# Graph layer and mixture of experts on one core: experts' rows split into 16-bit halves before they are turned

## The reference, cut to what matters

```python
x = x + gnn(layernorm(x), src, dst, edge_weight, ...)     # 3125 nodes x 256, 50000 edges
xt = layernorm(x)
# ffn, 8 experts, D = 256, H = 1024, the best 2 per node
probs = softmax(xt @ Wr + br)
top_p, top_idx = top_k(probs, 2)
weights = top_p / top_p.sum(-1)
xn = (xt - mu) * rsqrt(var + 1e-5)
xe = xn * ln_g[e] + ln_b[e]
h  = gelu(xe @ W1[e] + b1[e])                             # exact gelu
y  = h @ W2[e] + b2[e]
out = x + (weights * y[top_idx]).sum(over the 2)
```

## Time and profile before

| what | value |
|---|---|
| runs | 1226.39, 1227.84, 1229.69 us (median 1227.84) |
| the profiled execution | 1224.0 us |
| its span, first to last instruction | 1222.1 us |
| mean granted TensorE clock over the span | 0.818 |
| busy shares | TensorE 72%, VectorE 62%, GpSimd 54%, ScalarE 43% |

### The profile page before, as it was taken

The page is one execution under the profiler, slowest core; times in us unless marked ns, Lnnn a source line. Parts: engine busy times, 40 slices in busy tenths (PEclk is TensorE's granted clock), DMA queues, the critical chain, the costliest instruction groups (busy, mean ns, idle before and its releaser), DMA issues.

```text
span 1222.1 us, 26281 instructions
## 1 busy us (share of the span) xinstructions
PE 878.2 (72%) x6929; PEld 616.9 (50%) x6930; DVE 760.6 (62%) x1734; ACT 522.3 (43%) x1648; POOL 665.0 (54%) x668
## 2 busy tenths in 40 slices
PE   2284277658676556665579778884399999999994
PEld 1032043335333333333358656774287877877783
DVE  4666079766686556666466774897854555555552
ACT  7983168205463036640011003563055555555552
POOL 3844756564666666766667655351224454454543
PEclk9986589766778578988665769895599999999998
DMA  4114322234232233333444433453112323223231
GB/s 128 65 50 125 103 74 77 81 87 98 84 91 84 83 91 87 91 87 89 124 151 155 122 95 97 148 155 116 34 46 44 51 43 50 45 45 50 43 47 22
DMA packets 59615, 102.51 MB, mean 84 GB/s; under 512 B 10298, under 2 KB 43048, under 8 KB 59400
## 3 DMA queue, kind: packets, MB, share of 16 engines
q0 software_dynamic: 29520, 65.96, 22.4%
q1 hardware_dynamic: 30008, 35.55, 9.3%
HBM read 84.27 MB, written 17.20 MB: 83 GB/s over the span
## 4 chain that ended last, share of the span: by engine, by line
PE 38%; DVE 8%; issue 5%; DMA 1%; another core or an unknown queue 1%; DVEq 1%; ACT 1%; POOL 0%; POOLq 0%; ACTq 0%
PE bank L1061 8%; PE bank L1047 4%; PE bank L1048 4%; PE bank L1049 4%; PE bank L914 4%; PE bank L1063 3%; PE bank L901 2%; PE bank L903 2%; PE bank L902 2%; PE bank L987 1%; PE bank L997 1%; PE bank L1030 1%; DVE RA L1626 1%; DVE small L1694 1%
## 5 line engine op out<-in xcount | busy, mean ns | idle before, releaser
L738 POOL DMA_INDIRECT Wall<-xl_d,gbuf x391 | 396.3, 1013 | 236.3 <-SPq L606 111.4
L1155 ACT ACTIVATE Wall<-Wall 128x128 f32<-128x128 f16 (+1 forms) x782 | 230.3, 385 | 263.0 <-issue 138.2
L901 PE MATMUL bank<-Wall,RB 128*128 x488 | 167.2, 343 | 139.0 <-DVE Wall L1626 95.5
L1626 DVE TENSOR_TENSOR RA<-RA,bank 128x256 f32 x244 | 102.0, 418 | 203.7 <-remote 100.2
L792 POOL DMA_INDIRECT out_dram<-RA,slot_tok x56 | 100.7, 1798 | 163.0 <-ACT RA L1273 144.3
L1267 ACT ACTIVATE RA<-bank,b1T 128x128 f32<-128x128 f32 x448 | 128.1, 369 | 118.8 <-PE bank L1049 118.8
L1047 PE MATMUL bank<-RA,Wall 128*128 128x128 f16 x896 | 174.5, 220 | 0.4 <-issue 0.2
L1048 PE MATMUL bank<-RA,Wall 128*128 128x128 f16 x896 | 174.4, 220 | 0.0
L1049 PE MATMUL bank<-RA,Wall 128*128 128x128 f16 x896 | 174.3, 220 | 0.0
L1061 PE MATMUL bank<-Wall,RA 128*128 x448 | 169.1, 379 | 2.7 <-DVE RA L1905 0.9
L903 PE MATMUL bank<-Wall,RB 128*128 x488 | 167.3, 343 | 4.4 <-issue 4.4
(11 more groups left out here) (337 smaller groups left out, 1523.7 us busy)
## 6 DMA issues: line engine op xcount, KB each, us to landing
stage<-in_L_ffn_W SPq DMA_DIRECT2D x10, 1024.0 KB
Wall<-xl_d,gbuf POOLq DMA_INDIRECT x391
Wall<-in_L_ffn_W SPq DMA_DIRECT2D x6, 1024.0 KB, 6.5
Wall<-in_x SPq DMA_DIRECT2D x4, 640.0 KB, 6.7
xl_d<-Wall SPq DMA_DIRECT2D x4, 640.0 KB
out_dram<-RB SPq DMA_DIRECT2D x4, 640.0 KB
xn_d<-RA SPq DMA_DIRECT2D x4, 640.0 KB
RB<-in_x SPq DMA_DIRECT2D x1, 1792.0 KB
```

The source lines that it names most:

```text
L738: pool.indirect_dma_start(out=ring[:, t % RING * 2 * D:(t % RING + 1) * 2 * D], out_offset=None, in_=xl_d, in_offset=bass.IndirectOffsetOn ...
L901: mm(o, high, ring[:, bass.ds(at, D)], start=True, stop=False)
L1155: last = act.activation(hi_word[:, n % SR, k * S:(k + 1) * S], hi_hot[:, n // HB % 2, n % HB // 2, 0:S, n % 2], ACT.Copy, scale=pay[k][:, ...
L1626: dve.tensor_tensor(a, a, agg_out(n), ALU.add).then_inc(agg_added, 1)
```

## The change

The gathered float32 rows are split before they are turned. `row_highs` on ScalarE copies `xs` to a 16-bit tile; `row_lows` on VectorE subtracts that from `xs` for a second 16-bit tile; `turn` then makes four 16-bit transposes (two blocks of each half) in place of two float32 ones, against a 16-bit identity, into the same PSUM bank seen as 16-bit numbers. `x_high` reads the high halves from PSUM, and `x_low` becomes a plain copy of the low halves. `turn` waits for `row_lows` in place of the gather. The tiles of halves are two deep, in memory that was free. GpSimd makes the 16-bit identity in place of the zeros, once these have been stored.

```diff
+        xh_rows, xl_rows_x = [], []
+        for q in range(2):
+            for lst in (xh_rows, xl_rows_x):
+                lst.append(RA[:, at:at + D // 2].bitcast(F16))
+                at += D // 2
...
+            pool.wait_ge(spare_zeroed, 64)
+            pool.tensor_copy(ident_h, ident[:, :]).then_inc(ident_ready, 1)
             pool.wait_ge(slots_ready, 1)
-            pool.wait_ge(spare_zeroed, 64)
...
-            def turn(t, q, n):
-                pe.wait_ge(xs_in[q], 16 * n)
+            def turn(t, q):
+                pe.wait_ge(rows_lo, t + 1)
                 pe.wait_ge(fx_split, t + 1)
-                for kc in range(KC):
-                    m = nc.tensor.transpose(bank[6 + q % 2][:, kc * P:kc * P + P], xs[q][:, kc * P:kc * P + P], ident[:, :])
+                o = bank[6 + q][:, 0:D].bitcast(F16)
+                for half, rows in enumerate((xh_rows[q], xl_rows_x[q])):
+                    for kc in range(KC):
+                        at = half * D + kc * P
+                        m = nc.tensor.transpose(o[:, at:at + P], rows[:, kc * P:kc * P + P], ident_h)
                 m.then_inc(ft_mm, 1)
...
+            def row_highs(t, q, n):
+                act.wait_ge(xs_in[q], 16 * n)
+                act.wait_ge(ft_mm, t + 1)
+                act.activation(xh_rows[q % 2], xs[q], ACT.Copy).then_inc(rows_hi, 1)
+
             def x_high(t, q):
                 act.wait_ge(ft_mm, 2 + t + 1)
                 act.wait_ge(up_mm, 2 * t + 2)
-                act.activation(xhi[q], bank[6 + q][:, 0:D], ACT.Copy).then_inc(fx_hi, 1)
+                act.activation(xhi[q], bank[6 + q][:, 0:D].bitcast(F16)[:, 0:D], ACT.Copy).then_inc(fx_hi, 1)
...
+            row_highs(0, 0, 1)
+            row_highs(1, 1, 1)
             x_high(0, 0)
             x_high(1, 1)
+            row_highs(2, 2, 1)
             word = expert_word(0)
             gelu(0, 0, word, 0)
+            row_highs(3, 3, 1)
             x_high(2, 0)
             gelu(1, 1, word, 1)
             with act.Fori(0, FT // XR - 1) as i:
...
                     x_high(XR * i + q + 3, (q + 1) % 2)
                     gelu(XR * i + q + 2, q % 2, word, q + 2)
+                    row_highs(XR * i + q + 4, q, i + 2)
                     y_scale(XR * i + q, q % 2)
...
+            def row_lows(t, q):
+                dve.wait_ge(rows_hi, t + 1)
+                dve.tensor_tensor(xl_rows_x[q % 2], xs[q], xh_rows[q % 2], ALU.subtract).then_inc(rows_lo, 1)
+
             def x_low(t, q):
                 dve.wait_ge(fx_hi, t + 1)
-                dve.wait_ge(up_mm, 2 * t + 2)
-                dve.tensor_tensor(xlo[q], bank[6 + q][:, 0:D], xhi[q], ALU.subtract).then_inc(fx_split, 1)
+                dve.tensor_copy(xlo[q], bank[6 + q][:, 0:D].bitcast(F16)[:, D:2 * D]).then_inc(fx_split, 1)
...
             for c in range(2):
                 gate_hots(c)
+            row_lows(0, 0)
+            row_lows(1, 1)
             x_low(0, 0)
             x_low(1, 1)
+            row_lows(2, 2)
...
                     h_parts(XR * i + q + 1, (q + 1) % 2)
                     x_low(XR * i + q + 3, (q + 1) % 2)
+                    row_lows(XR * i + q + 4, q)
                     y_rows(XR * i + q, q % 2, word, q)
```

More of the change, by code:

```diff
@@ L226, in moe_gnn_program @@
             at += D
-        assert at <= NT * D
+        xh_rows, xl_rows_x = [], []
[3 more added lines that the diff above has]
+                at += D // 2
+        assert at <= (NT + 1) * D
         stages = [stage[:, :], f32view(Wall, (NE - 1) * WE // 2, KC * H)]
@@ L249, in moe_gnn_program @@
         zero_h = sb("zero_h", [P, 256], F16)
+        ident_h = zero_h[:, 0:P]
         one_h = sb("one_h", [P, 1], F16)
@@ L427, in moe_gnn_program @@
         ft_mm = sem("ft_mm")
+        ident_ready = sem("ident_ready")
+        rows_hi = sem("rows_hi")
+        rows_lo = sem("rows_lo")
         fx_hi = sem("fx_hi")
@@ L1085, in _ @@
             assert HC == 8
-            turn(0, 0, 1)
-            turn(1, 1, 1)
+            pe.wait_ge(ident_ready, 1)
+            turn(0, 0)
+            turn(1, 1)
             ex = experts(0)
@@ L1096, in _ @@
             m.then_inc(gates_mm, 1)
-            turn(2, 2, 1)
+            turn(2, 0)
             up(1, 1, ex[1])
@@ L1103, in _ @@
                 for q in range(XR):
-                    turn(XR * i + q + 3, (q + 3) % XR, i + 1 + (q + 3) // XR)
+                    turn(XR * i + q + 3, (q + 3) % 2)
                     up_and_down(XR * i + q + 2, q % 2, ex[q + 2], XR * i + q, q % 2, ex[q])
@@ L1109, in _ @@
                 if t + 3 < FT:
-                    turn(t + 3, (t + 3) % XR, (t + 3) // XR + 1)
+                    turn(t + 3, (t + 3) % 2)
                 if t + 2 < FT:
@@ L1927, in _ @@
             h_parts(0, 0)
+            row_lows(3, 3)
             x_low(2, 0)
```

## The result

The changed kernel took **1396.66 us** in the median of 4 runs (1395.71 to 1398.82), against 1228.76 us (1226.39 to 1229.84) for the kernel before: a ratio of 1.137, with a 95% interval from 1.135 to 1.140. It is slower, as forecast, but by 168 us where 113 were forecast, and it lies above the range of 1310 to 1390 us. The profiled executions are one each: 1395.71 us of the changed kernel, near its median, and 1224.0 us of the one before, 4.8 us under its median.

A forecast was written before the change was run, and what follows sets the result against it. TensorE was taken to bound the expert stage. 2.16 us a tile by 52 is 112.3, plus 1.2 for the stage's start: 113.5 us on 1224.0 gives 1337.5, and 3.8 to the median gives 1341 us; range 1310 to 1390.

The forecast's parts named there:

- What bounds the kernel: Expert stage: TensorE, busy 49.7 of 50 us at clock 1.00, is the bound; a tile takes 5.65 us.
- the new wait: Each of the loop's 52 turns waits for row_lows, behind row_highs, behind the last GELU half: +112.3 us.
- The ring's length: Expert loop, one turn to the next through TensorE, ScalarE and VectorE: 7.81 us a tile against 5.65; bounds 7.21 and 8.36.
- the term for TensorE's sequencer: After each turn in the loop, TensorE's register work and waits, hidden before, add 0.35 of a possible 0.63 us.
- the sum: Whole kernel: 112.3 us in the loop and 1.2 us before it make 113.5 us more.
- The turn itself: TensorE's transposes in each tile: four 16-bit ones take 0.22 us, two float32 ones 0.21; nothing gained.
- The third rival: Each transpose has a fixed price: four end 0.55 us later per tile, 29 us in all, 1370 us; chance 0.05.
- The fourth rival: Expert loop: halves ready a tile ahead, turns wait for nothing, 5.65 us a tile or 0.1 less; 1224 us, chance 0.04.
- x_high, x_low, gather, GpSimd: Expert stage: x_high and x_low gain or cost nothing, the earlier gather costs nothing, GpSimd's identity falls in its wait.
- The opening: Start of the expert stage: up(0) starts about 1.2 us later; nothing else is lengthened up to the loop.
- the second rival: TensorE's clock falls in the expert stage, 1.3 us a tile: half the tiles 34 us, 1375 us; all 1409; chance 0.28.
- the sum's bounds: Whole kernel: loop bounds of +81 and +141 us give 1310 to 1370 us.

The follow-up runs named there:

- The first experiment: The changed kernel with row_highs of tile T+4 moved ahead of the GELU of tile T+2, likewise for tile 3 before the loop: 1230.06 us.
- the last one: The kernel before with one wait added: in the loop, turn(T+3) waits for both GELU halves of tile T+1; 1315.50 us.
- the second experiment: The changed kernel with 12 extra matmuls of 256 columns, read by nobody, ahead of each turn of the loop: 1348.11 us.

## Why the prediction was wrong

**What bounds the kernel, and the new wait**: right. TensorE's next turn came to hang on the last GELU half, over ScalarE and VectorE, and undoing that with one moved line gives the time of the kernel before.

**The ring's length**: right within 0.1 us. It was put at 7.81 us and measures 7.90 where the clock holds. Term by term, with what was forecast in brackets: to the second GELU half 0.36 us (0.36), after its start 1.01 (1.03), the copy 0.43 (0.40), hand-over 0.04 (0.05), the subtraction 0.42 (0.41), to TensorE 0.06 (0.10). The 0.09 us that were missing are in the term for TensorE's sequencer, put at 0.35. In the tile shown it is 0.93 - 0.55 = 0.38, but over the 22 short tiles the last up matmul starts 5.59 us after the turn in place of 5.11 to 5.12, so 0.47 on average: 0.38 for the third and fourth tile of a round, 0.51 for the second and 0.58 at the head. The first experiment, whose turns don't wait, is back at 0.56 us from turn to first down matmul in three tiles of four, and the last one, whose turns do, has 0.92 to 1.11 us, by the place in the round. The price was read from a single row of the trace before, at the loop's start; without it the sum would have been another 18 us short.

**The turn itself**: right. Four 16-bit transposes take what two float32 ones took, 0.22 against 0.21 us to the first up matmul. The third rival, a fixed price for each, fell with that and with the first experiment's 1230.06 us. The Trainium skill ("TensorE: Matmul & The Clock Gate", Part 4: PE-mode transpose) gives about 275 ns for one in a kernel's context. Here each one's duration is 0.22 us, but the fourth starts 0.18 us behind the first (0.40 for all four), so a duration is no price in a row of them. The fourth rival, the chain off the path, is what the first experiment made: 5.62 us a tile, without the gain of 0.1 us that the rival had for faster transposes.

**x_high, x_low, gather, GpSimd**: right, as the first experiment shows for all of them at once. **The opening**: right for what it priced. From the first gather to up(0) it took 6.19 us before (877.42 to 883.61) and takes 7.35 now (881.95 to 889.30), 1.16 us more where 1.2 were forecast; from there to turn(3) another 0.4 us came, which had been put at nothing.

**The step that failed** is the assumption that the clock would stay at 1.00 through the stall: the fall of the clock was left out of the sum and kept as the second rival, and that rival was priced too low. I took the clock at 1.00 for the likeliest, at 0.60 against 0.28, and priced the rival at half of the tiles by 1.3 us. The trace showed 30 of 52 tiles and 1.62 us, 49 us in all, where the rival had 34; and with the stall filled, in the second experiment, just these 49 us are gone. The rows I had the earlier trace rows said that the clock bore an idle time of 1.04 us, bore one of 2.13 us once, and fell in one of 2.48 us, and I read the stall of nearly 2 us as being more likely on the safe side. That was single events set against a stall that comes 52 times. It was also too simple a reading of the last of them. A granted clock of 0.56 from 340 to 342 is 0.24 us at 1.00 and the rest at 0.50, so the clock fell near 340.24, and the idle time that ended at 341.60 had begun at 339.12: the clock fell about 1.1 us into it, 2.4 us behind the end of the one of 2.13 us. So these rows did not show that an idle time of 2.13 us is safe, nor that it takes 2.48. The price was low because I took it from the opening, where the matmuls ran at the low clock for 2.7 us after they had begun; in the tile shown above they run at it from 1060.0 to about 1063.4, with 0.31 us in place of 0.22 throughout. The range was drawn from the two parts side by side, the sum's bounds or the rival at half of its tiles. With the rival at the sizes that the runs show it would have been 1341 + 49 = 1390, and the 7 us that are left are the 0.09 us by which the ring was longer (5 us in 52 tiles), 0.4 us of the opening, and the 0.9 us between the two medians of the kernel before.

## What to carry to other kernels

Before an instruction is put into an engine's order, ask what the one in front of it waits for: behind a wait for the very work that is to come next on the bound engine it closes a ring, and the whole latency of the chain is paid at each pass (2.25 us a tile here), while the same instruction one place earlier was free. A stall on TensorE has a second price, the clock; where a stall can't be avoided, its idle time can be shortened by matmuls of no use: 12 of them gave back 49 us of 168 here, and 4 of them, 0.43 us in all, gave back 45. And a sequencer that has been held up shows its register work: count it into the ring.

## What the runs showed of the hardware that I had not expected

With a stall of 1.77 us in each tile of 7.9 us the granted clock fell to 0.50 in 30 tiles of 52, with 1.66 us in 26, with 1.32 us in none, and the fall can come behind the stall, when TensorE is busy again (1.2 us behind it in the tile shown). Eight transposes ahead of each turn kept it at 1.00 as eight matmuls of the same size did (1341.9 and 1343.8 us). And adding TensorE work to the changed kernel, whose TensorE stood waiting for the ring, made it 49 us faster.
